# Score products over 64 rows, two at a time, in a fused gated attention block

## What is computed

```python
# first block: 8 heads of 128; no softmax: cosine and variance scores against the context
x = x + tanh(g_xattn) * xattn(layernorm(x), ctx, ctx)
# second block: 16 heads of 16, batch of 32, S = 256
q, k, v = split_heads(z @ Wq), split_heads(z @ Wk), split_heads(z @ Wv)   # z = layernorm(x)
scores = einsum('bqd,bkd->bkq', q, k) / sqrt(256)
attn = softmax(scores, axis=-1)              # over q, for each key
out = einsum('bkq,bkv->bqv', attn, v)
z = l2norm(l2norm(out @ Wo) @ Wff)
x = x + tanh(g_ffn) * gelu(z)
```

## Time and profile before

| | us |
|---|---|
| median of 3 runs | 1452.59 (1451.85 to 1452.68) |
| the profiled execution, its own time | 1452.54 |
| its span, first to last instruction | 1450.8 |
| TensorE (PE) busy | 1305.6 |
| VectorE (DVE) busy | 1138.5 |
| ScalarE (ACT) busy | 1023.9 |
| POOL busy | 199.1 |
| one turn of the full loop | 72.5 |

### The profile page before, as it was taken

One profiled execution on the slowest core, in us unless ns is written; L12 is line 12 of the kernel. 1 busy time (PEld: TensorE's weight loads), 2 busy tenths in 40 slices (PEclk: granted clock), 3 DMA queues, 4 the chain that ended last, 5 costly groups with the idle time before them and its releaser, 6 DMA issues.

```text
span 1450.8 us, 35577 instructions
## 1 busy us (share of the span) xinstructions
PE 1305.6 (90%) x10818; PEld 878.3 (61%) x10818; DVE 1138.5 (78%) x3171; ACT 1023.9 (71%) x3381; POOL 199.1 (14%) x128
## 2 busy tenths in 40 slices
PE   4998838799999999999999999999999999999955
PEld 2565636566666666666666666666666666666621
DVE  5777545578888889888879787979787979797854
ACT  5565113368787878787878787878787878786866
POOL 2343041010202020202020202020202020202000
PEclk9999969899999999999999999999999999999987
DMA  8430001050606060605050505151515141514130
GB/s 265 140 109 18 1 13 46 26 160 5 170 11 166 15 164 16 162 19 160 21 156 25 156 25 147 33 151 30 147 34 142 38 140 41 136 44 130 39 117 15
DMA packets 151433, 124.52 MB, mean 86 GB/s; under 512 B 14462, under 2 KB 139039, under 8 KB 151392
## 3 DMA queue, kind: packets, MB, share of 16 engines
q1 hardware_dynamic: 151392, 124.00, 30.8%
HBM read 87.00 MB, written 25.77 MB: 78 GB/s over the span
## 4 chain that ended last, share of the span: by engine, by line
PE 38%; DVE 18%; issue 14%; ACT 6%; DMA 5%; SPq 3%; DVEq 1%; POOL 1%; ACTq 0%; POOLq 0%
PE work L861 10%; PE work L863 10%; PE work L862 10%; DVE nm L1627 5%; DMA sqE<-sq_rows 4%; PE attended L1347 4%; ACT prob L1437 3%; DVE mTl L1537 3%; PE score L1335 2%; SPq L1180 2%; DVE md L1582 2%; PE work L1242 1%; DVE l2s L1597 1%; DVE norm L1607 1%; DVE norm L1518 1%
## 5 line engine op out<-in xcount | busy, mean ns | idle before, releaser
L1437 ACT ACTIVATE prob<-score,nm 128x256 f32<-128x256 f32 x1024 | 473.2, 480 | 44.6 <-DVE nm L1627 40.4
L1627 DVE TENSOR_REDUCE nm<-score 128x2 f32<-128x512 f32 x512 | 340.2, 683 | 22.2 <-PE score L1335 20.0
L1437 ACT ACTIVATION_READ_ACCUMULATOR prob<-score,nm 128x1 f32 x1024 | 216.7, 212 | 0.0
L1335 PE MATMUL score<-qstack,kstack 128*128 128x256 f16 x1024 | 186.0, 277 | 28.4 <-ACT prob L1437 19.2
L1550 DVE BATCH_NORM_STATS2 qst<-work 128x6 f32<-128x128 f32 x512 | 112.6, 285 | 77.0 <-PE work L863 77.0
L1347 PE MATMUL attended<-prob,vsp 128*32 128x256 f32 x2048 | 139.4, 390 | 4.0 <-DVE vsp L1641 3.2
L1335 PEld LDWEIGHTS score<-qstack,kstack 128*128 128x128 f16 x1024 | 86.6, 98 | 87.7 <-ACT prob L1437 55.5
L861 PE MATMUL work<-woutTh,fvph 128*128 128x256 f16 x384 | 105.0, 273 | 13.7 <-DVE Vpl L1525 12.7
L1482 POOL TENSOR_TENSOR rq<-qft,mhalf 128x32 f32<-128x32 f32 x16 | 86.8, 5428 | 197.0 <-DVEq L1557 197.0
L1422 ACT ACTIVATE v<-work 128x512 f32<-128x512 f32 x32 | 19.1, 597 | 130.4 <-PE work L863 130.4
L862 PE MATMUL work<-woutTl,fvph 128*128 128x256 f16 x384 | 104.7, 273 | 0.0
(11 more groups left out here) (324 smaller groups left out, 3398.4 us busy)
## 6 DMA issues: line engine op xcount, KB each, us to landing
kstack<-parts SPq DMA_DIRECT2D x256, 64.0 KB, 2.9
qstack<-parts SPq DMA_DIRECT2D x256, 64.0 KB, 2.9
sqE<-sq_rows SPq DMA_DIRECT2D x64, 154.0 KB
s_xin<-in_x SPq DMA_DIRECT2D x8, 1024.0 KB, 6.0
xin<-in_x SPq DMA_DIRECT2D x16, 512.0 KB, 6.7
x2S<-in_x SPq DMA_DIRECT2D x16, 512.0 KB, 7.7
x<-x2S SPq DMA_DIRECT2D x16, 512.0 KB, 3.4
out<-zb SPq DMA_DIRECT2D x16, 512.0 KB, 3.4
```

What stands on the lines that cost most here:

```text
L1335: last = nc.tensor.matmul(sc[n % SC][:, jj * NQ:(jj + 1) * NQ], kstack[:, e, j, b2 * NQ + k * P:b2 * NQ + (k + 1) * P], qstack[:, j, b2 * ...
L1437: nc.scalar.activation(prob[:, g % PG, k, u % 4, :], sc[n % SC][:, jj * NQ:(jj + 1) * NQ], ACT.Exp, bias=nm[:, u:u + 1], accum_out=sums[:, ...
L1627: nc.vector.tensor_reduce(nm[:, 2 * n:2 * n + 2], sc[n % SC][:, :].rearrange("p (u q) -> p u q", q=NQ), AX.X, ALU.max, negate=True).then_i ...
```

## The change

The score step becomes four products of 64 rows: for two heads j, first rows 0 to 63 (e = 0) and then rows 64 to 127 (e = 1), into two different banks. There are 16 such steps, four score banks in two pairs, and a step waits until both its banks have been exponentiated. `kstack` loses its second copy and the zero rows, and POOL its memset. A group of the attended product is now a half k of the keys with both e (before: one e with both halves), so `vsp` and R change their layout. Both attended sums of a sequence lie in one bank, so each even P step waits until everything before is emptied. The number of M, X, R, P, E and L steps stays. SP waits for three memsets and not four. And the whole order is a new one.

```diff
-SC = 3
+SC = 4
 SCORES = 4 * GROUPS
 ORDER = """
-rk V0 qs1 G0 V0.h S0 qpow V1 G0.h M0 V0.l X0 G0.l S1 V1.h a1 M1 S2 S3 a1.h M2 G1 X1 V1.l G1.h M3 V2 ldr X2 a1.l S4
-V2.h qs2 S5 G1.l X3 a0 V2.l G2 M4 G3 a0.v M5 G2.h S6 aux X4 V3 R0 M6 G3.h G2.l X5 S7 P0 M7 V3.h G3.l G4 X6 sqe V3.l S8
-G5 G4.h M8 S9 X7 V4 G4.l M9 X8 R1 S10 X9 S11 M10 P1 G5.h X10 G5.l S12 V5 M11 ldy V4.h M12 S13 wq d0 X11 V4.l ldx V5.h
-M13 S14 X12 d1 V5.l R2 X13 M14 S15 P2 d0.o X14 M15 S16 m0.h d1.o fk0 M16 m0.l S17 fk0.h d2 E0 fk0.l d3 X15 M17 m1.h
-d2.o S18 X16 d4 m1.l M18 X17 R3 S19 d5 m2.h M19 X18 S20 m2.l P3 d3.o X19 d4.o fk1 m3.h M20 m3.l X20 S21 S22 z y0 m4.h
-fk1.h d5.o L0 m5.h M21 E1 R4 X21 M22 zT0 S23 m4.l X22 P4 fk1.l zT0.h m5.l S24 y0.o S25 y1 zT0.f M23 L1 X23 M24 M25 X24
-R5 X25 zT0.l zT1 y1.o O0 zT1.h ln1 S26 O0. S27 P5 zT1.f M26 lpow O1 M27 X26 ln2 X27 S28 S29 M28 O1. zz0 zz1 zT1.l
-zz0.h S30 R6 fk2 zz1.h zz0.l X28 P6 zz1.l fk2.h M29 S31 pk0 M30 X29 M31 X30 fk2.l pk1 X31 pq0 pk0.h R7 pk1.h pk0.l P7
-E2 pq0.h pk1.l L2 pq1 pq0.l E3 L3 O2 pq1.h pq1.l O3 O2. parts q0 O3. q1 F1 q0.o pv0 q1.o back0 F2 q2 pv0.v q3 q2.o F3
-q4 q3.o q5 q4.o q6 q5.o F4 q7 q6.o res pv1 back1 q7.o pv1.v out
+rk V0 qs1 V1 V0.h V0.l S0 qpow V1.h G0 M0 G1 G0.h V1.l S1 X0 M1 G2 G1.h G0.l X1 G1.l a1 M2 G2.h S2 a1.h V2 G2.l X2
+a1.l G3 qs2 V2.h wq M3 a0 G3.h V2.l a0.v M4 V3 X3 aux M5 ldx G3.l X4 ldr R0 S3 V4 V3.h M6 X5 M7 V3.l sqe X6 S4 V5 M8
+V4.h G4 M9 V5.h P0 V4.l X7 V5.l G5 G4.h R1 S5 X8 fk0 G4.l M10 M11 P1 fk0.h ldy z G5.h X9 fk1 X10 G5.l S6 fk0.l d0
+fk1.h M12 X11 M13 d1 E0 fk1.l X12 L0 R2 S7 X13 d2 d0.o M14 d3 m0.h d1.o m0.l m1.h S8 P2 M15 X14 m1.l X15 d4 d2.o M16
+m2.h d3.o d5 m2.l m3.h S9 M17 y0 X16 R3 M18 X17 m3.l X18 d4.o d5.o m4.h M19 S10 m5.h m4.l zT0 X19 P3 m5.l M20 zT0.h
+M21 S11 X20 y1 M22 E1 y0.o zT0.f L1 X21 M23 zT0.l X22 R4 zT1 y1.o X23 O0 ln1 zT1.h S12 zT1.f P4 O0. M24 lpow S13 fk2
+M25 X24 R5 X25 ln2 P5 fk2.h S14 zT1.l zz0 fk2.l zz1 zz0.h M26 q0 zz1.h zz0.l X26 M27 q1 zz1.l X27 q0.o pk0 E2 M28 M29
+X28 S15 pk1 q1.o pk0.h M30 X29 pq0 pk0.l X30 R6 M31 pq1 pk1.h L2 X31 pk1.l P6 pq0.h R7 pq1.h pq0.l P7 pq1.l O1 parts
+E3 L3 O2 O1. O3 O2. q2 O3. back0 q3 F1 q2.o pv0 q3.o F2 q4 pv0.v q5 q4.o F3 q6 q5.o q7 q6.o back1 pv1 q7.o F4 pv1.v
+out res
 """.split()
+def half(score):
+
+    group, i, e = score // 4, score % 4 // 2, score % 2
+    return group, e, 2 * i, 2 * (4 * group + 2 * e + i)
...
-    qstack, kstack = sb("qstack", [P, FH // 2, PR], F16), sb("kstack", [P, 2, FH // 2, PR], F16)
+    qstack, kstack = sb("qstack", [P, FH // 2, PR], F16), sb("kstack", [P, FH // 2, PR], F16)
-    pvb = [ps(f"attended{s}", [P, 512]) for s in range(2)]
+    pvb = ps("attended", [P, 2, NQ])
...
-            sp_wait(init, 4)
+            sp_wait(init, 3)
...
                 if kind == "S":
-                    (b2, t, e), k = unit(n // 4), n % 4 // 2
-                    if n % (SCORES // 2) == 0:
+                    (b2, t, k), i = unit(n // 2), n % 2
+                    if n % (SCORES // 4) == 0:
                         pe.wait_ge(stack_in[b2], b * 256 + 256 + START)
-                    pe.wait_ge(exp_done, b * 2 * SCORES + 2 * last_use(n, SC, SCORES) + 2 + EXP_CREDIT)
+                    pe.wait_ge(exp_done, b * 2 * SCORES + 2 * last_use(2 * n + 1, SC, SCORES) + 2 + EXP_CREDIT)
                     for jj in range(2):
-                        j = 4 * t + 2 * (n % 2) + jj
-                        last = nc.tensor.matmul(sc[n % SC][:, jj * NQ:(jj + 1) * NQ],
-                                                kstack[:, e, j, b2 * NQ + k * P:b2 * NQ + (k + 1) * P],
-                                                qstack[:, j, b2 * NQ:(b2 + 1) * NQ],
-                                                start=True, stop=True)
-                    last.then_inc(sc_ready, 1)
+                        j = 4 * t + 2 * i + jj
+                        for e in range(2):
+                            rows = slice(64 * e, 64 * e + 64)
+                            last = nc.tensor.matmul(sc[2 * i + e][:, jj * NQ:(jj + 1) * NQ],
+                                                    kstack[rows, j, b2 * NQ + k * P:b2 * NQ + (k + 1) * P],
+                                                    qstack[rows, j, b2 * NQ:(b2 + 1) * NQ], start=True, stop=True)
+                    last.then_inc(sc_ready, 2)
                 elif kind == "P":
...
                     if n % 2 == 0:
-                        pe.wait_ge(ot_done, b * 4 + n // 2 + 1)
-                    for k in range(KT):
+                        pe.wait_ge(ot_done, b * 4 + n // 2 + OT_CREDIT)
+                    for e in range(2):
                         for j in range(4):
...
                 elif kind == "M":
-                    dve.wait_ge(sc_ready, b * SCORES + n + 1 + SC_CREDIT)
+                    dve.wait_ge(sc_ready, b * SCORES + n // 2 * 2 + 2 + SC_CREDIT)
...
-            nc.gpsimd.memset(kstack[:], 0.0).then_inc(init, 1)
```

More of the change, by code:

```diff
@@ L911 @@
 EXP_CREDIT = 2 * SCORES
+VSTEP = 4 * 2 * FD + FD
 SC_CREDIT = SCORES
@@ L1203, in a_part @@
                             rows = slice(64 * e + FD * c, 64 * e + FD * (c + 1))
-                            for dst, n in ((kstack[rows, e, :, cols], 2 + c // 2), (qstack[rows, :, cols], c % 2)):
+                            for dst, n in ((kstack[rows, :, cols], 2 + c // 2), (qstack[rows, :, cols], c % 2)):
                                 src = parts[n].rearrange("(q e d) n -> e d q n", e=2, d=FD)[e][:, :, cols]
@@ L1317, in a_part @@
                     pe.wait_ge(rk_in, 32)
-                    nc.tensor.transpose(pvb[0][:, 0:P], md[:, 0, 0:P], ident[:])
-                    nc.tensor.transpose(pvb[0][0:KR_ROW, P:P + NB], md[0:NB, 1, 0:KR_ROW], ident[0:NB, 0:NB]).then_inc(rk_turned, 1)
+                    nc.tensor.transpose(pvb[:, 0, 0:P], md[:, 0, 0:P], ident[:])
+                    nc.tensor.transpose(pvb[0:KR_ROW, 0, P:P + NB], md[0:NB, 1, 0:KR_ROW], ident[0:NB, 0:NB]).then_inc(rk_turned, 1)
             def b_part(step, b):
@@ L1342, in b_part @@
                     pe.wait_ge(vs_ready, b * GROUPS + n + 1 + START)
                     if n % 2 == 0:
-                        pe.wait_ge(ot_done, b * 4 + n // 2 + 1)
-                    for k in range(KT):
+                        pe.wait_ge(ot_done, b * 4 + n // 2 + OT_CREDIT)
+                    for e in range(2):
                         for j in range(4):
-                            last = nc.tensor.matmul(pvb[t][32 * j:32 * j + 32, 0:NQ], vsp[:, e, k, j, :],
-                                                    prob[:, n % PG, k, j, :], start=(e == 0 and k == 0),
+                            last = nc.tensor.matmul(pvb[32 * j:32 * j + 32, t, :],
+                                                    vsp[:, k, (4 * e + j) * 2 * FD:(4 * e + j + 1) * 2 * FD],
+                                                    prob[:, n % PG, e, j, :], start=(e == 0 and k == 0),
@@ L1429, in b_part @@
                 if kind == "X":
-                    g, k = n // 4, n % 4 // 2
+                    g, e, j, u = half(n)
                     act.wait_ge(max_ready, b * SCORES + n + 1)
@@ L1435, in b_part @@
                     for jj in range(2):
-                        u = 2 * n + jj
-                        nc.scalar.activation(prob[:, g % PG, k, u % 4, :], sc[n % SC][:, jj * NQ:(jj + 1) * NQ], ACT.Exp,
-                                             bias=nm[:, u:u + 1], accum_out=sums[:, u:u + 1]).then_inc(exp_done, 1)
+                        nc.scalar.activation(prob[:, g % PG, e, j + jj, :], sc[n % SC][:, jj * NQ:(jj + 1) * NQ], ACT.Exp,
+                                             bias=nm[:, u + jj:u + jj + 1],
+                                             accum_out=sums[:, u + jj:u + jj + 1]).then_inc(exp_done, 1)
                 elif kind == "E":
@@ L1639, in b_part @@
                     dve.wait_ge(pv_done, b * GROUPS + n - 1 + PV_CREDIT)
[L1640 to L1642 removed]
+                    src = v[:, 2 * b2 + k, t * P:(t + 1) * P].rearrange("p (j e d) -> p e j d", e=2, d=FD)
+                    dst = vsp[:, k, :].rearrange("p (e x) -> p e x", x=VSTEP)[:, :, 0:4 * 2 * FD]
+                    nc.vector.tensor_tensor(dst.rearrange("p e (j y) -> p e j y", y=2 * FD)[:, :, :, 0:FD], src,
+                                            bc(sums[:, units].rearrange("p (e j) -> p e j", j=4).unsqueeze(3), [P, 2, 4, FD]),
                                             ALU.mult).then_inc(vs_ready, 1)
```

20 lines of the change are left out of this document (9 added, 11 removed).

## The result

| | before | after |
|---|---|---|
| median, us | 1452.22 (1448.39 to 1452.68, 4 runs) | **1428.71** (1425.69 to 1429.87, 4 runs) |
| profiled execution, own time / span | 1452.54 / 1450.8 | 1425.69 / 1424.0 |

The ratio is 0.9841, 95% interval 0.9818 to 0.9863: faster, 23.5 us in medians, where 12.5 were forecast.

A forecast was written before the change was run, and what follows sets the result against it. TensorE's queue was taken to bound each 72.5 us turn; -0.6 of its work and -0.3 of waits make -0.9 a turn, -13.5 us over 15, +1 for the end: from 1452.54 to 1440 us, range 1408 to 1476.

The forecast's parts named there:

- TensorE's sum, -0.6 a turn: TensorE's own work per turn: -3.4 us from overlapping score halves, +2.6 for shape changes, +0.2 for unhidden loads.
- 0.205 us for the two changes of shape: Gaps on TensorE before and after each score step, 0.09 plus 0.115 us, priced from the attended step; 16 steps, 3.3 us.
- the 8-column transpose: TensorE transpose at 749.76 that loses nothing beside full products; gave the lower bound, 0, for the price of shape changes.
- Rival 1: Shape changes around score steps cost next to nothing: TensorE -3.2 us, 1.0 back in waits, -2.2 a turn, near 1420 us; chance 0.20.
- rival 2: The score halves do not run side by side: steps keep 0.431 us, +2.5 us a turn, 1490 us; chance 0.09.
- The waits of the new order, -0.3 a turn: TensorE's waits per turn under the new order: +0.7 us at the head, -1.0 us in the rest.
- a turn of 71.6 us: Sign that the forecast is right: one loop turn shortened to 71.6 us, from 72.5 us.
- The head was to wait 2.0 us, +0.7: Start of the turn, V0 to V3: some 2.0 us of TensorE waits against 1.3 before.
- F4's new place: Final VectorE step, 1.2 us, moved behind q7.o: claimed to make the moments at the turn's head run 1.2 us later.
- the rest of the turn, -1.0: From d0 on: of 1.7 us of TensorE gaps 0.7 remain, and VectorE's wait for sqE should go.
- POOL's memset, "0, at most 2 us once": Removing GpSimd's kstack memset (6.92 us, in the first turn): gain 0, at most 2 us once.
- the end, +1: Last turn, where O1 now stands ahead of O2 at its end: +1 us once.

The follow-up runs named there:

- experiment 6: Kernel after with SyncE issuing the xin, ldr and wq loads earlier: 1425.21 and 1424.87 us; that kernel with all 128 rows in every score product: 1425.88 us.
- experiment 5: Kernel after with F4 moved back ahead of q7, all else kept: 1440.57 us, ratio to the kernel before 0.9899 to 0.9941.
- experiment 7: Kernel after with the early xin, ldr and wq loads, plus division R5 moved ahead of maximum M25: 1423.17 us, 1.7 from its control.

## Why the prediction was right, and where not

**TensorE's sum, -0.6 a turn: right.** Full overlap, 0.205 us for the two changes of shape, 0.5 spared by adjacent steps and 0.2 by P6 P7: the step costs 0.42 us, and the turn's busy time fell by 0.65 when the halves alone were changed. The row of the attended step was the right one to price from, and the 8-column transpose the wrong one. Rival 1 (changes free) would have shown 0.22 between full products, rival 2 (no overlap) 0.64.

**But it does not reach the end whole.** I added -0.6 to the waits' -0.3 as if they were independent. Taken alone, the halves gave 0.31 and the waits for VectorE took the rest. Rival 1 had this mechanism ("I give back 1.0 in new waits"), the forecast did not.

**The waits of the new order, -0.3 a turn: too small by a factor of two.** This is the term that failed. The new order with full rows takes 0.66 us off an undisturbed turn (experiment 6). In the sums of all 15 turns, 1084.76 and 1078.94 us against 1092.36 and 1096.29, it is anything from 0.5 to 1.2 us a turn, since they hold more or less waiting for sqE. With the halves' 0.31 the undisturbed turn lost 0.97 us where 0.9 was forecast. That the sum fits so well is luck: half of the -0.6 reached the end, and the order brought twice its -0.3. The sign that it had named, a turn of 71.6 us, was met: 71.57 and 71.88 on average in the two profiles of the kernel after. Two steps of the waits' working missed. The head was to wait 2.0 us, +0.7; the brackets in the timeline show less:

```profile
729.84 0.24 PE L861 MATMUL work<-fvph,wNh 128*128 128x154 f16 x1 [0.20 <-DVE Vpl L1533]
...
730.99 0.60 PE L1294 MATMUL work<-ident,aux 128*8 128x128 f32 x4 [0.56 <-DVE Gl L1545]
...
734.20 0.28 PE L861 MATMUL work<-woutTh,fvph 128*128 128x256 f16 x1 [0.31 <-DVE Vpl L1533]
```

With the 0.06 to 0.16 us that each restart adds, 1.4 us in all: no loss against the 1.3 of before. The places were right (a1 on Gl, V3 on V2.l), the lengths were not, since V0.l started 3.5 us behind V0 and not 3.8. F4's new place, which I charged for it, is the better one (experiment 5). And the rest of the turn, -1.0: the scores' and the zz transposes' waits went as foreseen, but that the wait of VectorE for sqE "should go" was wrong. It was 12.6 us over 12 turns before, and 7.6 and 11.7 after in its two profiles, with xin and x2S in the queues beside it. I had seen xin go ahead of sqE and priced it at 0; taking it out of the way, with the two small loads, gave 7.6 us in experiment 6. P5's wait was named in the text ("late anyhow") and not priced; experiment 7 shows that it could not have been had for itself.

**POOL's memset, "0, at most 2 us once": wrong.** Moving the memset alone gave 3.9 us in the first turn, enough for all of the 3.5 of the kernel after. I looked for who waits for GpSimd by a semaphore, found nobody, and did not look at VectorE's row beside it, where a copy of eight columns takes 5.71 us.

**Small terms:** the end, +1 (measured 0); no wait of score steps for their two banks among the four largest of the 12 turns; P steps on the one attended bank 2.2 us in the whole run, 0 forecast. From the forecast of 1440 us to the profiled execution's 1425.69 it is 14.3 us: 4.6 are the setup's chance, 3.5 the memset, 18.8 - 13.5 = 5.3 the turns, 1 the end. Of the 5.3 the undisturbed turn explains 1; the other 4 are mostly sqE, less late in this profile than in the one before, and the second profile of the kernel after gives 14.1 us in place of 18.8. The median of the four runs stands 3.0 above that execution.

**Open:** the order's 0.66 us rests on a single undisturbed turn of the kernel before, and two profiled runs of one kernel differ by 3 to 6 us in their 15 turns, mostly by how late sqE is. Which of the order's moves brought it was not tried one by one, F4 apart.

## What to carry to other kernels

Splitting the array pays by the stretch, not by the product: each change of shape costs about 0.1 us, as much as a full product of 256 columns, so gather what has one shape, and price a split by start to start including both edges. Where three engines are over 90% busy, expect work taken from one to come back in part as waits for another: here about half of it did. And let a load go as soon as its buffer is free: here, loads that travelled beside a needed transfer made turns of uneven length, and moving them ahead took most of that away.

## What was not expected

- Matmuls on the two row halves run side by side even when two of one half are issued before the other's: 0.33 us against 0.32.
- A memset of GpSimd held VectorE's copies and normalizations in SBUF for its whole length: 5.77 us for a copy of 0.16, 8.13 for four normalizations of 1.59. VectorE's rows looked busy, not waiting.
- Undisturbed turns repeat to 0.01 us (71.23 and 71.24), finer than medians of six runs, which move by some us. A difference of 0.3 us a turn can be read there and not in the totals.
